# Diagonal linear-attention states and token-wise denominators, with two splits moved to other slots, in a fused attention kernel on one core

## The reference

```python
q, k = elu(xn @ wq) + 1, elu(xn @ wk) + 1; v = xn @ wv      # per head
S_kv += k_t v_t^T ; z += k_t                                # over the tokens t
out_t = (q_t S_kv) / (q_t . z + 1e-6)
linear = out @ wo

q, k, v = xn @ Wq.T + bq, xn @ Wk.T + bk, xn @ Wv.T + bv     # per head
q = (q / |q| + query_embedding) * softplus(temperature)
h = softmax(q k^T / sqrt(32)) v
gated = h * (sum of gates from two softmaxes and a top 3)
out = x + linear + gated @ Wp.T + bp
```

## Time and profile before

| | |
|---|---|
| median of 3 runs | 4007.16 us (4003.08 to 4007.56) |
| the profiled execution | 4005.88 us, span 4004.0 us |
| TensorE busy | 3778.7 us, 94% |
| VectorE busy | 3404.7 us, 85% |
| ScalarE busy | 2743.9 us, 69% |
| GpSimd busy | 396.6 us, 10% |
| granted TensorE clock | mean 0.989; full through all steps with attention |
| DMA | 316.62 MB, 79 GB/s |

### The profile page before, as it was taken

The page is one execution under the profiler, slowest core; times in us unless marked ns, Lnnn a source line. Parts: engine busy times, 40 slices in busy tenths (PEclk is TensorE's granted clock), DMA queues, the critical chain, the costliest instruction groups (busy, mean ns, idle before and its releaser), DMA issues.

```text
span 4004.0 us, 143634 instructions
## 1 busy us (share of the span) xinstructions
PE 3778.7 (94%) x63871; PEld 1724.8 (43%) x63872; DVE 3404.7 (85%) x3532; ACT 2743.9 (69%) x2809; POOL 396.6 (10%) x229
## 2 busy tenths in 40 slices
PE   2789999999999999999999999999999999999999
PEld 1544444444444444444444444444444444444333
DVE  5668989889898988888898888889788788888887
ACT  2457777777777777677777677677677676767663
POOL 3100000000001001101101101110000000110120
PEclk8889999999999999999999999999999999999999
DMA  5322212222223223223222323323222222322223
GB/s 208 102 81 60 72 45 70 60 70 56 58 82 88 73 72 103 73 67 96 78 77 78 91 64 90 93 61 92 68 60 79 77 71 58 93 66 59 75 83 116
DMA packets 366756, 316.62 MB, mean 79 GB/s; under 512 B 159449, under 2 KB 314553, under 8 KB 365493
## 3 DMA queue, kind: packets, MB, share of 16 engines
q1 hardware_dynamic: 365412, 298.98, 25.5%
q10 hardware_dynamic: 720, 8.39, 0.5%
HBM read 231.26 MB, written 76.01 MB: 77 GB/s over the span
## 4 chain that ended last, share of the span: by engine, by line
PE 79%; ACT 12%; issue 3%; DVE 2%; DMA 1%; SPq 1%; ACTq 0%; POOL 0%; DVEq 0%; POOLq 0%
PE ps L1072 33%; PE ps L1228 19%; PE ps L1214 18%; ACT prob L904 11%; PE ps L1131 3%; PE ps L1111 2%; PE ps L1152 1%; PE ps L1158 1%; SPq L430 1%; DMA rq<-rq_scratch 1%; ACT r L847 1%; PE ps L1195 0%; DVE acc L1758 0%; DMA xlo_scratch<-xt_lo 0%; PE ps L1164 0%
## 5 line engine op out<-in xcount | busy, mean ns | idle before, releaser
L904 ACT ACTIVATE prob<-ps 128x2048 f32<-128x2048 f32 x1024 | 1924.8, 1880 | 544.4 <-PE ps L1214 541.8
L1758 DVE TENSOR_TENSOR acc<-acc,prob 128x2048 f32<-128x2048 f32 x896 | 2057.8, 2297 | 95.9 <-ACT prob L904 76.5
L1228 PE MATMUL ps<-prob,v 128*32 128x512 f32 x8192 | 1091.4, 605 | 0.4 <-issue 0.4
L1214 PE MATMUL ps<-q_hi,k_hi 32*128 32x512 f16 x4096 | 422.8, 384 | 107.1 <-ACT prob L904 103.0
L1072 PE MATMUL ps<-x_hi,w_hi 128*32 128x512 f16 x4096 | 412.5, 383 | 2.6 <-ACT rdl L857 2.3
L1214 PE MATMUL ps<-q_lo,k_hi 32*128 32x512 f16 x4096 | 413.1, 374 | 1.1 <-issue 0.9
L1214 PE MATMUL ps<-q_hi,k_lo 32*128 32x512 f16 x4096 | 413.0, 374 | 0.1
L1072 PE MATMUL ps<-x_lo,w_hi 128*32 128x512 f16 x4096 | 411.7, 381 | 0.0
L1072 PE MATMUL ps<-x_hi,w_lo 128*32 128x512 f16 x4096 | 411.6, 381 | 0.0
L1228 PEld LDWEIGHTS ps<-prob,v 128*32 128x32 f32 x8192 | 161.2, 107 | 434.2 <-issue 434.2
L1072 PE MATMUL ps<-wop_hi,fin 128*32 128x512 f16 x4096 | 342.5, 380 | 4.3 <-DMA y<-in_x 2.6
(11 more groups left out here) (261 smaller groups left out, 4550.8 us busy)
## 6 DMA issues: line engine op xcount, KB each, us to landing
x_hi<-xhi_scratch SPq DMA_DIRECT2D x64, 512.0 KB, 6.5
x_lo<-xlo_scratch SPq DMA_DIRECT2D x64, 512.0 KB, 7.9
x_in<-in_x SPq DMA_DIRECT2D x64, 256.0 KB, 7.4
rq<-rq_scratch SPq DMA_DIRECT2D x64, 256.0 KB
rdl<-rdl_scratch SPq DMA_DIRECT2D x64, 256.0 KB
y<-in_x SPq DMA_DIRECT2D x64, 256.0 KB, 6.0
out<-y SPq DMA_DIRECT2D x64, 256.0 KB, 5.9
rden<-rden_scratch SPq DMA_DIRECT2D x63, 256.0 KB
```

What stands on the lines that cost most here:

```text
L904: s_.activation(prob[i % 3][:], ps[:, 0:HG, :], ACT.Exp, bias=-SHIFT, scale=inv_c[:, g:g + 1] if wide else 1.0 / CQK).then_inc(exped, 2)
L1214: last = t_.matmul(bank[h], kk[rows32(h), cols128(kt)], qq[rows32(h), :], start=(kk is kh and qq is qh), stop=(kk is kl and not wide))
L1228: last = t_.matmul(bank[OUT][rows32(h), :], v[m // NB % 2][:, kt, rows32(h)], prob[i % 3][:, h, :], start=(kt == 0), stop=(kt == TT - 1))
L1758: v_.tensor_tensor(acc[:], acc[:], prob[i % 3][:], ALU.add).then_inc(summed, 1)
```

## The change

It has four parts. Key-values are multiplied for the diagonal blocks alone, so `kvm` and `st` have 32 columns and no zeros, one ScalarE copy replaces four, and the state products have 32 rows. The linear denominators are made with the tokens on the partitions (16 products of 4 columns). ScalarE copies 128x16, VectorE inverts that, and TensorE turns it in slot 1 (`turn_dl`). VectorE copies the turned 16x128 in slot 2 (`keep_rdl`), and `pack` with its two DMAs is gone. The queries of the first three blocks of a group are scaled and split in slot 2 of the next step, with two buffers `qb`. `divide_h` and ScalarE's `split_h` stand in slot 7, VectorE's `split_h` in slot 8.

```diff
+def deferred(s):
+    n = prepared(s)
+    return n if n is not None and n % NB < NB - 1 else None
...
-        blockden, ones_v = sb("blockden", [P, P]), sb("ones_v", [P, HD])
+        heads_v, ones_v = sb("heads_v", [P, HG]), sb("ones_v", [P, HD])
...
# SyncE
                     if kt == 0:
-                        if p is not None:
-                            sp.wait_ge(dl_kept, p + 1)
-                            pack(rdl_c, rdl_d, rdl, dl_out, dl_in, p)
...
                         if p is not None:
-                            sp.wait_ge(rdl_done, p + 1)
+                            sp.wait_ge(rdl_kept, p + 1)
                             spread(rdl, rdl_d, rdl_c[:], rdl_out, rdl_in, p, o1_ready)
# ScalarE
             def keep_dl(p):
                 act.wait_ge(dl_mm, p + 1)
-                act.wait_ge(o1_ready, p)
-                s_.activation(rdl[:], X1, ACT.Identity, bias=eps1[:, 0:1]).then_inc(dl_kept, 1)
+                act.wait_ge(rdl_turned, p)
+                s_.activation(dl[:].rearrange("p h t -> p t h"), X1[:, 0:BT * HG].rearrange("p (t h) -> p t h", t=BT), ACT.Identity,
+                              bias=eps1[:, 0:1]).then_inc(dl_kept, 1)
...
-                for h in range(HG):
-                    ins = s_.activation(kvm[rows32(h), :, h, :], X1[rows32(h), :].rearrange("p (t n) -> p t n", t=BT)[:, :, rows32(h)],
-                                        ACT.Copy)
-                ins.then_inc(kv_kept, 1)
+                s_.activation(kvm[:].rearrange("p t e -> p (t e)"), X1[:, 0:BT * HD], ACT.Copy).then_inc(kv_kept, 1)
...
+                    if kt == 2 and deferred(s - 1) is not None:
+                        split_q(deferred(s - 1))
...
-                    if kt == 9 and mp is not None:
+                    if kt == 7 and mp is not None:
                         split_h(mp)
...
-                    if kt == 12 and n is not None:
+                    if kt == 12 and n is not None and deferred(s) is None:
                         split_q(n)
# TensorE
             def linear_den(n):
                 pe.wait_ge(pz_ready, n + 1)
-                t_.matmul(X1, blockden[:], zc[:], start=True, stop=True).then_inc(dl_mm, 1)
+                for j in range(BT):
+                    last = by_columns(X1[:, j * HG:(j + 1) * HG], zc[:, cols128(j)], heads_v[:], True, True)
+                last.then_inc(dl_mm, 1)
+
+            def turn_dl(p):
+                pe.wait_ge(rdl_done, p + 1)
+                t_.transpose(X0[0:HG * BT, 0:P], dl[:].rearrange("p h t -> p (h t)"), ident[:]).then_inc(rdl_turned, 1)
...
                 for j in range(BT):
-                    last = by_columns(X1[:, cols128(j)], pk[:, j, :], vl[:, j, :], True, True)
+                    for h in range(HG):
+                        last = t_.matmul(X1[rows32(h), j * HD:(j + 1) * HD], pk[:, j, rows32(h)], vl[:, j, rows32(h)],
+                                         start=True, stop=True)
...
                     for h in range(HG):
-                        last = t_.matmul(X1[rows32(h), cols128(j)], st[:, i % NST, rows32(h)], phqT[:, cols128(j)], start=False, stop=True,
-                                         skip_group_check=True)
+                        last = t_.matmul(X1[rows32(h), cols128(j)], st[rows32(h), i % NST, :], phqT[rows32(h), cols128(j)], start=False,
+                                         stop=True, skip_group_check=True)
...
                             pe.wait_ge(am_ready, 2 * p + 2)
+                            turn_dl(p)
...
+                    if kt == 2 and p is not None:
+                        pe.wait_ge(rdl_kept, p + 1)
# VectorE
             def invert_dl(p):
-                dve.wait_ge(dl_in, (p + 1) * 16)
-                v_.reciprocal(rdl_c[:], rdl_c[:]).then_inc(rdl_done, 1)
+                dve.wait_ge(dl_kept, p + 1)
+                v_.reciprocal(dl[:], dl[:]).then_inc(rdl_done, 1)
+
+            def keep_rdl(p):
+                dve.wait_ge(rdl_turned, p + 1)
+                dve.wait_ge(rdl_out, p * 16)
+                v_.tensor_copy(rdl_c[:], X0[0:HG * BT, 0:P]).then_inc(rdl_kept, 1)
...
+                    if kt == 0 and p is not None:
+                        invert_dl(p)
...
                     if kt == 2:
                         if p is not None:
-                            invert_dl(p)
+                            keep_rdl(p)
...
+                        if deferred(s - 1) is not None:
+                            scale_q(deferred(s - 1))
...
+                    if kt == 2 and deferred(s - 1) is not None:
+                        split_q(deferred(s - 1))
...
-                    if kt == 8 and mp is not None:
+                    if kt == 7 and mp is not None:
                         divide_h(mp)
...
-                    if kt == 11 and n is not None:
+                    if kt == 11 and n is not None and deferred(s) is None:
                         scale_q(n)
-                    if kt == 12 and mp is not None:
+                    if kt == 8 and mp is not None:
                         split_h(mp)
-                    if kt == 13 and n is not None:
+                    if kt == 13 and n is not None and deferred(s) is None:
                         split_q(n)
```

More of the change, by code:

```diff
@@ L300, in build @@
         a3 = cursor[0]
-        qb, sq = sb("qb", [P, BN]), sb("sq", [P, BN])
+        qb, sq = [sb(f"qb{i}", [P, BN]) for i in range(2)], sb("sq", [P, BN])
         rq_c, rq = sb("rq_c", [HG * BT, P]), sb("rq", [P, BN])
@@ L308, in build @@
         am = sb("am", [P, HG, BT, P])
-        st = sb("st", [P, NST, P])
-        kvm = sb("kvm", [P, BT, HG, HD])
-        rdl_c, rdl, o1 = sb("rdl_c", [HG * BT, P]), sb("rdl", [P, BN]), sb("o1", [P, BN])
+        st = sb("st", [P, NST, HD])
+        kvm = sb("kvm", [P, BT, HD])
+        dl, rdl_c, rdl, o1 = sb("dl", [P, HG, BT]), sb("rdl_c", [HG * BT, P]), sb("rdl", [P, BN]), sb("o1", [P, BN])
         o_hi, o_lo = sb("o_hi", [P, BN], F16), sb("o_lo", [P, BN], F16)
@@ L356, in build @@
         o_stored, h_stored = sem("o_stored"), sem("h_stored")
-        den_out, den_in, rden_out, rden_in, dl_out, dl_in, rdl_out, rdl_in, rq_out, rq_in = (
-            sem(n) for n in ("den_out", "den_in", "rden_out", "rden_in", "dl_out", "dl_in", "rdl_out", "rdl_in", "rq_out", "rq_in"))
+        den_out, den_in, rden_out, rden_in, rdl_out, rdl_in, rq_out, rq_in = (
+            sem(n) for n in ("den_out", "den_in", "rden_out", "rden_in", "rdl_out", "rdl_in", "rq_out", "rq_in"))
         settled, pool_const, dve_link, act_const, pool_pow = (
@@ L365, in build @@
             sem(n) for n in ("wsq_ready", "n2_done", "n2_kept", "ak_ready", "whi_split", "wlo_split"))
-        e_turned, setup_done, kvm_cleared, headmask_ready = (sem(n) for n in ("e_turned", "setup_done", "kvm_cleared", "headmask_ready"))
+        e_turned, setup_done, headmask_ready = (sem(n) for n in ("e_turned", "setup_done", "headmask_ready"))
         ln_stat, ln_pow, ln_done, x_summed = sem("ln_stat"), sem("ln_pow"), sem("ln_done"), sem("x_summed")
@@ L381, in build @@
             sem(n) for n in ("ql_proj", "kl_proj", "ql_part", "kl_part", "phq_done", "phk_done", "phk_turned", "pk_kept"))
-        scan_done, pz_ready, dl_mm, dl_kept, rdl_done = (sem(n) for n in ("scan_done", "pz_ready", "dl_mm", "dl_kept", "rdl_done"))
+        scan_done, pz_ready, dl_mm, dl_kept, rdl_done, rdl_turned, rdl_kept = (
+            sem(n) for n in ("scan_done", "pz_ready", "dl_mm", "dl_kept", "rdl_done", "rdl_turned", "rdl_kept"))
         at_done, am_ready, kv_done, kv_kept, state_ready, num_done, num_kept, o1_ready, ohi_done, olo_done = (
@@ L804, in keep_q @@
                 g = n // NB % NG
-                act.wait_ge(qlo_done, n)
-                s_.activation(qb[:], X1, ACT.Identity, bias=bqs[:, g:g + 1], scale=1.0 / XS).then_inc(qb_done, 1)
+                if n > 1:
+                    act.wait_ge(qlo_done, n - 1)
+                s_.activation(qb[n % 2][:], X1, ACT.Identity, bias=bqs[:, g:g + 1], scale=1.0 / XS).then_inc(qb_done, 1)
             def keep_ss(n):
@@ L821, in split_q @@
                 act.wait_ge(qs_done, n + 1)
-                s_.activation(q_hi[n % NRING][:], qb[:], ACT.Identity, bias=c2[:, g:g + 1]).then_inc(qhi_done, 1)
+                s_.activation(q_hi[n % NRING][:], qb[n % 2][:], ACT.Identity, bias=c2[:, g:g + 1]).then_inc(qhi_done, 1)
             def split_k(n):
@@ L934, in step @@
                         keep_ss(n)
+                    if kt == 2 and deferred(s - 1) is not None:
+                        split_q(deferred(s - 1))
+                    if kt == 2 and n is not None:
                         split_k(n)
@@ L1665, in scale_q @@
                 dve.wait_ge(qb_done, n + 1)
-                v_.tensor_tensor(qb[:], qb[:], rq[:], ALU.mult).then_inc(qs_done, 1)
+                v_.tensor_tensor(qb[n % 2][:], qb[n % 2][:], rq[:], ALU.mult).then_inc(qs_done, 1)
             def split_q(n):
@@ L1671, in split_q @@
                 dve.wait_ge(qhi_done, n + 1)
```

(2 more changed lines are left out.)

7 lines of the change are left out of this document (2 added, 5 removed).

## The result

| | before | after |
|---|---|---|
| median of the runs | 4006.22 (4003.08 to 4007.56) | 3962.64 (3959.66 to 3965.3) |
| profiled execution, its span | 4005.88, 4004.0 | 3964.83, 3963.0 |
| ratio | | 0.9892, 95% interval 0.9875 to 0.9909 |

What follows compares the result with a forecast made beforehand. TensorE was taken as the bound, its matmuls filling 3778.7 of 4004.0 us. 60 x (-0.61 - 0.53 + 0.08) = -63.6, first steps -8, late loads +4 and +11 gave -56.6: 3950.6 us, range 3930 to 3985 (8 in 10).

Steps and rivals of the forecast that it cites:

- Slots 15, 13 and 1: Per-step terms: denominators save 0.61 us, narrow key-values save 0.53, the added transpose costs 0.08; over 60 steps -63.6 us.
- rival (c): Small products cost per instruction, not per column, so the 60 steps win nothing: 4014 us, slower by 0.2%; chance 3%.
- (d): The 32x32 state products of slot 3 don't run side by side, 2.6 us more a step: 4110 us; chance 3%.
- Slot 3: State products keep count and columns, and their change of tile shape moves ahead of them: nought, bounds 0.12 us either way.
- if slot 3 grows: One of the signs named beforehand that would show the prediction wrong: slot 3, with the state products, gets longer.
- Slots 11 to 14 get room, but the exponential loop or TensorE sets them already: Moving query work to the next step's slot 2 frees these slots but gains nothing there; cost also nought.
- Rival (e): The slot 13 gain isn't taken because the next exponential or key-query's inputs are next: 3982 us; chance 5%.
- Late loads in the middle: Broadcast loads landing late for the softmax-output division in slot 7 hold up ScalarE's next exponential: +4 us in all.
- Rival (b): Loads late in most steps, up to 4027 us; 5% for a cost over 30 us, 2% of it beyond nought.
- The last four steps: Shorter slots make the division's load late: stalls of 1.0, 1.7, 4.2 and 4.2 us, 11 in all, called certain.
- First steps: Steps without attention gain from fewer query-factor waits, cheaper denominators and a smaller copy: 8 us, bounds 4 and 14.
- the 4 us that the sum had for the deferral: In steps without attention, three of four waits behind the query-factor broadcast (7.1 us in four) go: 4 us saved.

## Why the prediction was right, and where it missed

- **Slots 15, 13 and 1**: right. -0.66, -0.56 and +0.07 a step for -0.61, -0.53 and +0.08. The 16 products of 32 columns take 0.44 us and those of 4 columns 0.37, so rival (c) is out; the state products take 1.01 us, so (d) is out too. What slot 15 gave beyond its term is the change of shape: behind the 4-column products it costs 0.04 us (0.37 against the 0.33 of the earlier trace rows, behind which the shape stays), for 0.12 in the sum. By the rule of the Trainium skill (TensorEngine Tiling, Instruction Overhead) 32 instructions taken one after another would need 0.80 us, an estimate. The trace's 0.37 and 0.44 us disagree with that, as the row of before did.
- **Slot 3**: mis-sized, at the edge of its bounds, and the prediction's own sign of being wrong ("if slot 3 grows") came true. The change of shape did not move from behind the state products to ahead of them: there are two now. 0.13 us a step, 8.0 in all, for nought. The step from 32x32 back to the scores' 32x128 costs what the one from 128x32 did.
- **"Slots 11 to 14 get room, but the exponential loop or TensorE sets them already"**: the step that failed, though the total hides it. It is true of before. Once key-values is short, VectorE's output addition is next, and the moves are what keeps it out of the way. The gain from that room was put at nought; without either move slots 13 and 14 of steps 16 to 59 give 10.3 us less than with the splits back alone. That kernel, at 3966.2, is only 3.6 us above after, because in after the late loads take most of this gain back. Rival (e) gave the wait 5%, for the right reason (the moves make room); that reason belonged in the sum as a gain of theirs.
- **Late loads in the middle**: +6.1 for +4, right in kind; the size is in part chance, as the spread above shows. Their cause wasn't seen: the prediction counted issue times of before, and what makes them late is the block load, as the run with it in slot 9 shows. Rival (b) named the right chain.
- **The last four steps**: +21.1 for +11, the largest error. In step 62 the division's chain needed 3.13 us for the store (1.35 in before, from 3878.09 to the issue in the earlier trace rows) and 5.74 for the load (5.29 taken): the exponential came 1.8 + 0.45 us later than worked out. That is slot 8, 6.2 us longer. Then slot 9 took 2.8 us more, since TensorE's clock was at half after its idle. The sum had no term for what an idle of 6 us does to the engine behind it. Why the store took longer there isn't tested. The traces narrow it down: beside the store of step 62 a 16 KB packet of kind instruction starts 0.7 to 0.9 us after its issue in each of the eight kernels that have the token-wise denominators and this store in its old place, where it takes 2.7 to 3.3 us. The four kernels without those denominators have no such packet there, nor have the two with the early reciprocal, and all six stores take 1.35 us.
- **Behind the last exponential**: -5.6 us, given back, unforeseen. The 6.2 us of store and load that stand there in the chain of before are gone from the chain of after.
- **Slots 4 and 5**: +6.1 us, unforeseen. That the breaks come with the block load is shown twice (16.0 to 2.1 and 11.9 to 2.4 us when it moves). That TensorE waits there for its instructions, which the profile shows as packets on the DMA engines, fits the end of 167 of 169 breaks just behind a packet of kind instruction; no run took those packets away, so this stays inferred. The rise goes with the token-wise denominators: the kernel with them alone has 19 breaks in those slots, before and the three kernels without them 7 to 10. It has 31 matmuls a step more; how that leads to more breaks is not settled, and the load was not moved in the kernel before.
- **First steps**: -8.3 for -8, with luck: in kernels with the same first steps this stretch ran from -5.8 to -10.2. The denominators alone give -9.5, so the 4 us that the sum had for the deferral are not shown.

The forecast's -56.6 and the -41.0 found differ by 15.6: +8.0 slot 3, +6.1 slots 4 and 5, +2.1 slots 8 and 9, +10.1 at the end, -5.6 behind it, +0.4 in the other slots, and -5.5 for what slots 1, 13, 14 and 15 and the first steps gave beyond their terms. The range held the time partly because these misses have both signs.

## What to carry to other kernels

Before a part is costed at nought, ask what is next once another part of the same change is in: a move that frees an engine can be worth nothing alone and decide what a shorter product brings beside it. A late load is priced with what it leaves behind, here TensorE's clock, and looked for at its start: the small store ahead of it, and the bulk transfers that share its engines. Where these can be issued some slots later at no cost, that is the cheapest gain in reach; here one moved line brought 13 and 16 us (medians), as much as the narrow key-values alone.

## What the runs showed of the hardware

- 32 matmul instructions of 32 columns take 0.41 us and of 4 columns 0.37 us (medians of after, from the first start to the start of what follows in another shape). Eight times the columns cost 0.04 us.
- A change of tile shape behind products of 128 or 512 columns costs about 0.12 us (0.99 against 0.87, 1.00 against 0.88), also from 128x32 to 32x32: slot 3 is 0.13 longer with two than with one. Behind products of 4 columns it costs 0.04 us (0.37 against 0.33).
- TensorE came back from 6.14 us of idle at half its clock: the mean granted clock was 0.52 from 3838 to 3845, and it worked from 3839.25.
- 167 of 169 breaks within TensorE's products in slots 4 and 5, over 14 traces, end 1.15 to 1.65 us behind the end of a 16 KB packet of kind instruction.
- A store of 8 KB lands in 1.36 us, and in 5.20 us where 1 MB of loads was issued 5 us ahead of it (1319.26 and 1319.67 in the queue of after; the store at 1324.13).
